# Two transformer blocks with experts: three chunks in the first group, and a delta-rule state laid out by key

## The reference

```
def step(W, inputs):
    k_i, v_i, q_i, b_i = inputs
    v_bar = jnp.einsum('bhvk,bhk->bhv', W, k_i)
    W = W + jnp.einsum('bhv,bhk->bhvk', b_i * (v_i - v_bar), k_i)
    y = jnp.einsum('bhvk,bhk->bhv', W, q_i)
    return (W, y.reshape(B, H * dk))
```

## Time and profile before

| | us |
|---|---|
| runs (median; lowest, highest) | 1880.94; 1879.56, 1885.45 |
| the profiled execution | 1881.02 |
| its span | 1878.5 |
| busy: TensorE, VectorE, ScalarE, POOL | 1385.0, 1092.9, 855.8, 840.6 |

### The profile page before, as it was taken

How to read it: one execution, slowest core, us unless ns; L and a number is a source line. 1 busy time by engine, 2 the same in 40 slices (tenths; PEclk the granted TensorE clock), 3 DMA queues, 4 the chain that set the end, 5 groups by cost and what they waited for, 6 DMA issues and landing times.

```text
span 1878.5 us, 29132 instructions
## 1 busy us (share of the span) xinstructions
PE 1385.0 (74%) x8304; PEld 1046.0 (56%) x8304; DVE 1092.9 (58%) x2573; ACT 855.8 (46%) x1811; POOL 840.6 (45%) x826
## 2 busy tenths in 40 slices
PE   2788998846377878777777787785554999945986
PEld 1355555523135666666656667574443777844764
DVE  3677777635626781122766455757688757793144
ACT  1466666634125434464644455643131645312543
POOL 2011111105777761557835743646757451382043
PEclk9999889978679979888887887987786999967998
DMA  7654544349124434343434332423101021111123
GB/s 306 180 146 142 152 137 138 89 156 376 65 69 148 148 119 123 110 120 113 134 93 120 110 89 79 126 73 124 43 20 50 29 68 32 32 43 41 35 78 97
DMA packets 226295, 204.43 MB, mean 109 GB/s; under 512 B 21372, under 2 KB 197269, under 8 KB 223093
## 3 DMA queue, kind: packets, MB, share of 16 engines
q1 hardware_dynamic: 197699, 150.31, 25.8%
q0 software_dynamic: 22528, 42.78, 7.6%
q10 hardware_dynamic: 5938, 9.69, 1.4%
HBM read 95.87 MB, written 106.82 MB: 108 GB/s over the span
## 4 chain that ended last, share of the span: by engine, by line
PE 39%; DVE 15%; POOL 9%; issue 8%; ACT 7%; DMA 1%; SPq 0%; DVEq 0%; POOLq 0%; ACTq 0%
PE psum L1235 6%; PE psum L1305 5%; PE psum L1256 4%; PE psum L1289 4%; PE psum L1379 4%; PE psum L1400 3%; POOL sorted_x L2050 3%; PE psum L1247 3%; POOL w_all L2108 2%; POOL e_gath L2063 2%; ACT e_gath L1523 2%; PE psum L1387 2%; PE psum L1225 2%; PE psum L1156 1%; PE psum L1162 1%
## 5 line engine op out<-in xcount | busy, mean ns | idle before, releaser
L2063 POOL DMA_INDIRECT e_gath<-sorted_y,e_rowsy x256 | 280.7, 1096 | 261.1 <-issue 129.9
L2050 POOL DMA_INDIRECT sorted_x<-h_fm,e_rows x256 | 269.5, 1053 | 121.3 <-issue 77.3
L1770 DVE TENSOR_TENSOR e_a<-psum,e_g 128x176 f32<-128x176 f32 x224 | 75.4, 338 | 312.1 <-ACT e_g L1480 298.8
L1235 PE MATMUL psum<-w_all,e_xd 128*128 x896 | 227.6, 366 | 8.4 <-issue 3.9
L298 DVE TENSOR_REDUCE at_negm<-psum 128x2 f32<-128x512 f32 x256 | 163.2, 684 | 67.6 <-PE psum L174 66.8
L1235 PEld LDWEIGHTS psum<-w_all,e_xd 128*128 128x128 f32 x896 | 160.1, 219 | 43.9 <-issue 37.9
L1305 PE MATMUL psum<-ident,e_prod 128*128 128x128 f32 x640 | 143.2, 388 | 47.1 <-DVE e_prod L1822 47.1
L1305 PEld LDWEIGHTS psum<-ident,e_prod 128*128 128x128 f32 x640 | 141.7, 312 | 48.9 <-DVE e_prod L1822 47.6
L1247 PE MATMUL psum<-ident,e_a 128*88 128x128 f32 x448 | 99.7, 308 | 75.7 <-DVE e_a L1770 37.6
L375 ACT ACTIVATE w_all<-psum 128x512 f32<-128x512 f32 x256 | 141.7, 591 | 26.9 <-PE psum L187 22.3
L1480 ACT ACTIVATE e_g<-psum 128x176 f32<-128x176 f32 x224 | 71.6, 320 | 159.7 <-PE psum L1235 158.4
(11 more groups left out here) (299 smaller groups left out, 2802.9 us busy)
## 6 DMA issues: line engine op xcount, KB each, us to landing
sorted_y<-e_ys SPq DMA_DIRECT2D x134, 256.0 KB, 2.2
e_xt<-sorted_x SPq DMA_DIRECT2D x112, 256.0 KB, 2.7
sorted_x<-zeros SPq DMA_DIRECT2D x10, 2048.0 KB
qk_parts<-at_part SPq DMA_DIRECT2D x96, 192.0 KB, 3.3
at_qs<-qk_parts SPq DMA_DIRECT2D x16, 576.0 KB
at_ks<-qk_parts SPq DMA_DIRECT2D x16, 576.0 KB
sorted_x<-zeros ACTq DMA_DIRECT2D x16, 512.0 KB
w_all<-in_w_all SPq DMA_DIRECT2D x1, 7296.0 KB, 24.2
```

Of the source, the lines that this page charges most:

```text
L1235: mm = pe.matmul(ps[:, UP[p % 2], i * 256:i * 256 + 2 * HIDDEN], x_d[:, q % 2, t % 4 * P:(t % 4 + 1) * P], w_all[:, ds(offset[t], 2 * HIDD ...
L2050: pool.indirect_dma_start(sorted_x, bass.IndirectOffsetOnAxis(rows0[:, t, k:k + 1], 0), h_tm[:, t * D:(t + 1) * D], None).then_inc(scatter ...
L2063: pool.indirect_dma_start(gath[:, t % GATH, k * D:(k + 1) * D], None, sorted_y[g], bass.IndirectOffsetOnAxis(rows_y[:, t, k:k + 1], 0)).th ...
```

## The change

- Chunks are sorted in groups of 3, 3 and 2 in place of 2, 3 and 3. The layer-0 tiles are 448 as before, with the boundaries of the groups at pairs 80 and 160 (64 and 144 before). The opening routes three chunks before its first ranking, and POOL scatters 96 transfers, not 64, before the first tile.
- The recurrence starts later for chunk 0 and runs closer: `BEGIN` and `STEP` below. Chunks 0 to 3 lie in the 224 ticks with pairs (0 to 2 before).
- The state is laid out `[z][key][head][value]`. A sum over the key index begins with `FOLDS[m]` halvings on VectorE (`fold`, additions of the upper half to the lower, 1024, 512, 256 and 128 wide), and TensorE adds the 16 / 2^folds slices that are left, for the key sums too (`key_sum`, `query_sum`); the slices are contiguous. Outer product and update are one operation of 2048 for each `z` in place of two of 1024.
- The second layer's tokens are sorted in four groups, of 4, 2, 1 and 1 chunks (40, 24, 16 and 16 tiles in place of 40, 32 and 16).
- The layer-0 gathers of chunks 6 and 7 go into the buffers of the second layer's gathers, one for each tile; ScalarE's scaling of them has ticks of its own (`SCALE`).
- Two layer norms of a chunk are normalised by ScalarE (`act_norm`), with factors that VectorE forms, not by VectorE (L742).
- Turning back, mix and result of chunks 0 to 6 stand between the tiles of the last group.

```diff
-GROUP0 = ((0, 2), (2, 5), (5, 8))
+GROUP0 = ((0, 3), (3, 6), (6, 8))
...
-SORTED = ((0, 4), (4, 7), (7, 8))
+SORTED = ((0, 4), (4, 6), (6, 7), (7, 8))
...
-Y_ON_PE = 3
-BEGIN = (97, 135, 179, 219, 243, 267, 291, 316)
-STEP = (19, 20, 20, 12, 12, 12, 12, 12)
+BEGIN = (114, 144, 171, 199, 227, 255, 276, 299)
+STEP = (14, 13, 13, 13, 11, 10, 9, 9)
...
-SCATTER1 = (155, 195, 237, 257, 298, 315, 336, 358)
-BEGIN1 = (271, 331)
+SCATTER = ((28, 33, 43, 46), (46, 50, 54, 71))
+SCATTER1 = (170, 188, 214, 237, 267, 292, 312, 340)
...
+FOLDS = (4, 3, 3, 3, 4, 2, 1, 0)
...
+BEGIN1 = (251, 298, 330)
+GATHER1 = (296, 333, 353)
...
-        state = sb("state", [P, LT, HEADS, DEPTH, KD])
-        prod = sb("prod", [P, LT, HEADS, DEPTH, KD])
+        state = sb("state", [P, LT, KD, HEADS, DEPTH])
+        prod = sb("prod", [P, LT, KD, HEADS, DEPTH])
...
+        LATE = CT * GROUP0[2][0]
+        GATH_HOME = [("gath", t % GATH, t - GATH if t >= GATH else None) for t in range(LATE)]
+        GATH_HOME += [("rows", i, None) for i in range(TILES - LATE)]
...
+            def key_sum(m, s, z):
+                n, left = CB * m + s, KD >> FOLDS[m]
...
+                for k in range(left):
+                    mm = pe.matmul(side[:, (LT + z) * P:(LT + z + 1) * P], ident[:], prod[:, z, k].rearrange("p h v -> p (h v)"),
+                                   start=(k == 0), stop=(k == left - 1))
+                mm.then_inc(vbar_done, 1)
...
+            def query_sum(m, s, z):
...
+                for k in range(left):
+                    mm = pe.matmul(side[:, z * P:(z + 1) * P], prod[:, z, k].rearrange("p h v -> p (h v)"), ident[:],
+                                   start=(k == 0), stop=(k == left - 1))
                 mm.then_inc(y_done, 1)
...
+                if op == "fold_query" or op == "fold_key" and n > 0:
+                    left = KD >> (part + 1)
...
+                    v.tensor_tensor(pr_z[:, 0:left], pr_z[:, 0:left], pr_z[:, left:2 * left], ALU.add).then_inc(folded, 1)
...
-            for m in range(CHUNKS):
-                turn_back(m)
+            for t in range(FIRST_TILE1[NG1 - 1], FIRST_TILE1[NG1] + 2):
+                stage1(t, FIRST_TILE1[NG1 - 1], TILES1[NG1 - 1])
+                if t - FIRST_TILE1[NG1 - 1] in BACK_AT:
+                    turn_back(BACK_AT[t - FIRST_TILE1[NG1 - 1]])
+            turn_back(CHUNKS - 1)
```

More of the change, by code:

```diff
@@ new lines, with pieces_of_chunk, products, update @@
+SCATTER = ((28, 33, 43, 46), (46, 50, 54, 71))
+SCATTER1 = (170, 188, 214, 237, 267, 292, 312, 340)
+FOLDS = (4, 3, 3, 3, 4, 2, 1, 0)
+HALVES = (0, 1)
+SUM_LAG = 1
+def pieces_of_chunk(m):
+    def products(op, s, z):
+        return tuple((op, s, z, half) for half in HALVES) + tuple(("fold_" + op, s, z, level) for level in range(FOLDS[m]))
+    def update(s):
+        return tuple((op, s, z, 0) for z in range(LT) for op in ("outer", "add"))
+    keys = [tuple(x for z in range(LT) for x in products("key", s, z)) for s in range(CB)]
+    return (keys[0] + (("u", 0, 0, 0),) + update(0)
+            + keys[1] + products("query", 0, 0) + (("u", 1, 0, 0),) + products("query", 0, 1) + update(1)
+            + products("query", 1, 0) + products("query", 1, 1))
@@ new lines, in ticks_of_chunk @@
+def ticks_of_chunk(m):
+    pieces, n = pieces_of_chunk(m), CB * STEP[m]
+    weight = [2 if x[0] in ("outer", "add") else 1 for x in pieces]
+    ticks, last, at = [[] for _ in range(n)], {}, 0
+    for i, (op, s, z, part) in enumerate(pieces):
+        at = max(at, sum(weight[:i]) * n // sum(weight))
+        needs = [("key", s, y) for y in range(LT)] if op == "u" else [("query", 0, z)] if op == "outer" and s > 0 else []
+        at = min(n - 1, max([at] + [last[x] + SUM_LAG for x in needs]))
+        ticks[at].append((op, s, z, part))
+        last[op.replace("fold_", ""), s, z] = at
+    return ticks
@@ new lines, in sums_of_chunk @@
+def sums_of_chunk(m):
+    ticks = ticks_of_chunk(m)
+    last = {}
+    for i, pieces in enumerate(ticks):
+        for op, s, z, _ in pieces:
+            last[op.replace("fold_", ""), s, z] = i
+    last["query", 0, 0] = max(last["query", 0, 0], last["u", 1, 0])
+    sums, tick = [], 0
+    for op, s in (("key", 0), ("key", 1), ("query", 0), ("query", 1)):
+        for z in range(LT):
+            tick = max(tick, last[op, s, z] + SUM_LAG)
+            sums.append((tick, op, s, z))
+    return sums
@@ L1320, in jobs @@
                         project(m, p - PROJECT[m])
[L1321 to L1327 removed]
+                    for tick, op, i, z in SUMS[m]:
+                        if r == tick and op == "key" and CB * m + i > 0:
+                            key_sum(m, i, z)
+                        if r == tick and op == "query":
+                            query_sum(m, i, z)
                     if e == 3:
@@ L1793, in piece @@
[L1793 to L1808 removed]
+                queries, keys = phi[:, n % PHI_BUFS, z, 0], phi[:, n % PHI_BUFS, z, 1]
@@ L1822, in piece @@
[L1822 to L1832 removed]
+                    dve.wait_ge(added, LT * n + z + 1)
@@ L2025, in _ @@
                     if 0 <= p - BEGIN[m] < CB * STEP[m]:
-                        recurrence(m, (p - BEGIN[m]) // STEP[m], (p - BEGIN[m]) % STEP[m])
+                        for op, s, z, part in PIECES[m][p - BEGIN[m]]:
+                            piece(m, op, s, z, part)
                 jobs(p)
-            for m in range(SORTED[1][1]):
+            for m in range(CHUNKS - 1):
                 mix(m)
-            for m in range(SORTED[1][1]):
-                result(m)
-            for m in range(*SORTED[2]):
-                mix(m)
-                result(m)
+                if m > 0:
+                    result(m - 1)
+            result(CHUNKS - 2)
+            mix(CHUNKS - 1)
+            result(CHUNKS - 1)
         @block.gpsimd
```

311 lines of the change are left out of this document (165 added, 146 removed), and 8 rows, old and new, of the table OPENING.

## The result

The changed kernel takes 1889.11 us (median of 20 runs, 1878.77 to 1896.39), the kernel before 1879.39 in 20 runs beside it: ratio 1.0055, 95% interval 1.0036 to 1.0074. It is 10 us slower, where 23 us faster was forecast. The range, 1822 to 1893, holds the time; the sign is wrong.

What follows compares the result with a forecast made beforehand. Bound in turn by pairs and recurrence coupled tick by tick, recurrence alone, and late layer-1 tiles. Terms +46 - 81 - 18 + 24 + 6 = -23 took 1881 to 1858 us; range 1822 to 1893.

Steps and rivals of the forecast that it cites:

- the overhead in ticks 114 to 225: Pairs beside recurrence: 114 us above TensorE's sum of 316, at 0.39 of VectorE's time; stretch taken as 426 us.
- Rival 1: Ticks 114 to 224: VectorE paces the pairs, products wait behind updates and halvings; 471 us there, 1903 in all; chance 0.20.
- Norms to ScalarE: Recurrence beside pairs: normalising moves from VectorE to ScalarE at no cost; without ScalarE's slack, 3 us a chunk.
- the opening: Before the first pair: three chunks and 96 scatters put the first pair at about 582 us, +24.
- the durations of updates and of contiguous sums: Recurrence: 2048-wide updates take 2.3 us; contiguous sum matmuls 0.24 us each against 0.45 with strided weights.
- both engines' sums in the pair ticks: Ticks 114 to 225: busy time of 316 us for TensorE and 293 us for VectorE.
- Rival 3: Sums on TensorE: contiguous ones are no faster, 47 us more, about 38 on the path; 1896 us; chance 0.05.
- Rival 2: Pairs beside recurrence stay smooth, overhead stays per tick at 84 us; stretch 400 us, 1832 in all; chance 0.20.
- rival 4: POOL or the new gather buffers hold the chain by 20 us or so; about 1880 us, no change; chance 0.05.
- ticks 225 to 251: Between pairs and layer-1 tiles: only chunk 4's recurrence is left, 108 us against 189, -81; bounds 92 and 123.
- the ticks up to 114: Pairs before recurrence: tick 80 at about 789 us, tick 114 at 888, from a first pair at 582.
- From the first layer-1 tile to the group of 24 tiles: Layer-1 tiles from tick 251: 170 us for 40 tiles to tick 293, then 18 us of waiting for token rows.

Runs made afterwards that it cites:

- Norms first: Changed kernel with only the norms' statistics and factors moved ahead of the recurrence's pieces on VectorE; ratio 0.9921 to the kernel before.
- jobs first: Changed kernel with all short jobs of the chunks ahead of the recurrence's pieces on VectorE in each tick; ratio 0.9922 to the kernel before.

## Why the prediction was wrong

*The step that failed* is the overhead in ticks 114 to 225: "Before, 97 us of the 431 lay above TensorE's sum, 0.39 of VectorE's time. The same share now is 114". It was 455.0 - 316.4 = 139 us, 0.48 of VectorE's time. The share was taken over as if it were a property of the two engines; most of what it grew by comes from the order on VectorE. With 2.66 us of VectorE's work a tick in place of 1.95, jobs of 0.2 us waited behind up to 5.4 us of pieces, and TensorE, which takes its own jobs in program order, stood with its pairs behind them. Norms first brings 427 us, and 1861.57 us in all against 1858 forecast. That this hits both forecasts is in part luck: the overhead is then 427.1 - 304.8 = 122 us, 0.42 of VectorE's time, still above the forecast's 114, and TensorE's busy time lies 11 us under its sum of 316 because its clock is higher.

*Rival 1* came nearest: it decides "from 4.1 us a tick upward", and 455 us over the 109 ticks from the product of tick 114 to that of tick 223 is 4.17. Its mechanism, products behind updates, is real: product waits rose from 18.1 to 41.4 us, and a cut of 56 to 58 us of VectorE's work took 26 and 20 us. But it is not what turned the sign: with norms first the product waits are still 41.3, and 25 us are gone.

*Norms to ScalarE* I cost at nothing, with ScalarE's slack as the cover. It cost 13 us here. The cover was counted in busy time, which doesn't see that one hop more between engines means one wait more for a turn. That this is how the 13 us arise is argued, not shown: with the norms back on VectorE, waits for norms fell by 4 us and TensorE's busy time by 6, at a granted clock of 0.82 in place of 0.81.

*Right:* the opening (first pair at 582.6, forecast 582; 575.4 in the second profile, so the hit to a microsecond is luck); the last of 256 scatters ended at 795.5 and the first gather began at 798.4 (forecast 801 and 802); the durations of updates and of contiguous sums; both engines' sums in the pair ticks, TensorE's at the clock of this order. Rival 3 is out by the sum rows. Rival 2 did not come: no kernel with the new schedule took 400 us or less there. Of rival 4 the first gather came on time, but the order of POOL's gathers had a price that the sum lacked: in the profile, 10 us of the stretch behind the pairs.

*Right in number, in part wrong in reason:* ticks 225 to 251, 108 us forecast, 114 measured. I took VectorE to be the bound, and 12 us less of its work shortened the stretch by 5. The long wait for a norm there, 24.2 us, is not what sets its length: jobs first took it to 3.2 us, TensorE waited up to 20.5 us for the recurrence's product in its place, and the stretch became 125 us in place of 118. Norms first left 18.5 us of it, since the factors still stand behind the routing of the tick before, and the stretch is 119.

*Off in size:* the ticks up to 114 took 316 us from the first pair where 306 were forecast. Six of these 10 us are a slip in the forecast's own sum: 34 ticks at 102 / 33 are 105 us, which from 789 gives 894 and not 888. The other 4 lie between a pair's first matmul and its product (558.3 and 562.3 in the kernel before), which the forecast took as one time. From the first layer-1 tile to the group of 24 tiles it took 203 where 188 were forecast, and from there to the last group 156 where 176. Together with the first that is 5 us, and they weren't tried apart.

## What to carry to other kernels

Two engines, each about two thirds busy and coupled tick by tick, take a time that their busy sums don't give: read from the trace which short instruction of a chain over several engines stands behind long independent work in an in-order queue, and put it first. A share of overhead measured in one schedule can't be carried to a denser one without looking at that order. And try the same edit on the kernel before: here it gained 9 us without the rest of the change, against 25 with it, and nothing in the old schedule with the new layout.

## What the runs showed that was not expected

Two executions of one kernel with spans of 1894.6 and 1887.4 us agree within 0.1 us from the product of tick 0 to the end, and differ by 7.0 us in when POOL's first scatter starts (455.28 and 448.31 us). Nearly all of their difference arises ahead of that scatter. And removing a wait of 24.2 us, the longest single wait of its stretch, gained nothing there: with jobs first it shrank to 3.2 us, a wait of 20.5 for another product of VectorE came up, and the stretch was 6 us longer.
